# Adding layer 2's direct outputs over the dimensions on GpSimd in place of VectorE, and dealing the gathers out 9, 10, 11, 9 a block

## The chip, the cores and the metric

The kernel runs on one core of a Trainium2 chip. The metric is the device time of one execution in microseconds (us). Three executions of the kernel before took 1320.02, 1320.3 and 1326.73 us, median 1320.3.

## The reference

1024 samples each have 39 ids. Each id picks a row of 16 floats from one of 39 tables, which gives x0 of shape (1024, 39, 16). Three layers follow, all in float32:

```
for idx, (W, b) in enumerate(params):          # W: (39, fields of xk, 128)
    z = einsum('bhd,bkd,hks->bsd', x0, xk, W) + b
    z = relu(z)                                 # (samples, 128 units, 16 dimensions)
    layers 0 and 1: xk = z[:, :64], direct gets z[:, 64:]
    layer 2:        direct gets all 128 units of z
logit = sum(concatenate(direct, axis=1), axis=-1)   # over the 16 dimensions
```

The logit (64 + 64 + 128 = 256 numbers a sample) and 16 dense inputs go through a small network: 272 to 512, 512 to 256, 256 to 1, with relu after the first two.

## The kernel before, in words

**Tiles and blocks.** The samples are cut into 8 blocks of 128. A tile is one block times 4 of the 16 dimensions, so that it has 512 columns (4 dimensions by 128 samples), and there are 32 tiles, t = 0 to 31, 4 to a block. The units lie on the 128 partitions. One body of the loop (37 us) handles tile t: layer 1 of t, layer 0 of tile t + 1, layer 2 of t, and the transposes of the gathered rows for tile t + 2 (AHEAD = 2). Every engine has its own program with the same bodies in the same order (`steps`, line 329): the first bodies are written out, then comes a hardware loop whose turn is 4 bodies, then the rest is written out again. GpSimd's loop has one turn less than the others.

**Products.** In layers 1 and 2 there are 10 steps j = 0 to 9, each of two products of 128 x 512. VectorE multiplies (line 687) and TensorE contracts (line 789). The table KINDS says how a step reaches TensorE:

```
KINDS = {1: "UVPPUPVPVP", 0: "UUUU", 2: "UUVUPUVPUP"}
```

A U step goes to TensorE as it is, as two float32 matmuls. A V or P step is split in a rounded head (ScalarE, line 559) and a rest, which is the product minus its head; then TensorE makes six shorter matmuls. The rest of a V step is made by VectorE (line 694), the rest of a P step by GpSimd (line 464). So GpSimd makes the rests of j = 2, 3, 5, 7, 9 of layer 1 and of j = 4, 7, 9 of layer 2. TensorE takes the steps in order and waits for each P step on `s_rest_p`.

**The queue of GpSimd.** Between its rests, GpSimd issues the gathers of a later block, one indirect DMA for each of the 39 fields (`gather`, line 449), into the tile `gathered`. GATHERS_OF_TILE says how many a body issues, by k = (t + 2) mod 4, and GATHERS_AFTER how many of them may follow the n-th rest of a layer; what is left over goes after the last rest of layer 2:

```
GATHERS_AFTER = {1: (0, 1, 0, 0, 7), 2: (1, 2, 2)}
GATHERS_OF_TILE = (11, 12, 12, 4)
```

So a body with t mod 4 = 2 has k = 0 and 11 gathers, t mod 4 = 3 has 12, t mod 4 = 0 has 12 and t mod 4 = 1 has 4. In the body with k = 0, GpSimd first waits until ScalarE has copied the previous block's rows away, and copies the new block's indices (`refill`, line 504, `new_indices`, line 444). That body gathers nothing before the last rest of layer 1. From t = 26 on there is nothing left to gather. ScalarE waits for all 39 gathers of a block at line 573, in layer 1 of the body with t mod 4 = 2.

**The direct outputs.** ScalarE writes relu(z) of layer 2, transposed in its access pattern, to 4 of the 16 dimensions of `direct2` (128 units x 128 samples x 16 dimensions; `out_layer2`, line 563, called in layer 1 of the next body). When the 4 tiles of a block are in, VectorE adds the 16 dimensions with one tensor_reduce over 2048 columns and writes 128 columns of `sum2`:

```
def add_dims(out, direct, t, done):
    nc.vector.tensor_reduce(cols, direct[:], AX_X, ALU.add).then_inc(done, 1)
```

For layer 2 this is `add_layer2` (line 720). It stands in the body of VectorE with t mod 4 = 0, between the products of layer 0 and the wait for layer 2's input x2 (`s_x2`), for t = 4 to 28, and once more at the end of its program. The directs of layers 0 and 1 have `add_layers01` (line 724), in layer 2 of the body with t mod 4 = 3, after step j = 7; it is not touched. Two others wait for `s_sum2`: ScalarE, before it writes the first tile of the next block into `direct2` (line 566, in layer 1 of the body with t mod 4 = 1), and TensorE in the network at the end (line 857), where the first 512 samples need 4 sums and the second 512 need all 8.

Of the kernel before, what the change touches and what calls it, by code (L numbers as in the profile page):

```python
# [8 lines left out]
ALU = mybir.AluOpType  # L9
# [3 lines left out]
P = 128  # L13
FIELDS = 39
# [20 lines left out]
PE_ORDER = {1: (0, 1, 2, 3, 4, 5, 6, 7, 8, 9), 2: (0, 1, 2, 3, 4, 5, 6, 7, 8, 9)}  # L35
WHOLE_SLOTS = 6
SPLIT_SLOTS = 4
GATHERS_AFTER = {1: (0, 1, 0, 0, 7), 2: (1, 2, 2)}
GATHERS_OF_TILE = (11, 12, 12, 4)
GATHERS_EARLY = (20, 10, 9)  # L40
D2_AFTER = 6
XT_AFTER = 3
# [7 lines left out]
TOGETHER = TPB  # L50
D0_AFTER = 5
AHEAD = 2


class Tile:
# [30 lines left out]
def build_kernel(nc, dense_ctx, ids, tables, W_top1, b_top1, W_top2, b_top2, W_top3,  # L86
# [3 lines left out]
    TILES = BLOCKS * TPB  # L90
# [14 lines left out]
    with ExitStack() as ctx:  # L105
# [6 lines left out]
        def sem(name):  # L112
            return ctx.enter_context(nc.semaphore(name))
# [28 lines left out]
        idx = sb("idx", [P, FIELDS], I32)  # L142
# [61 lines left out]
        s_select = sem("first_shift_selected")  # L204
        s_ids = sem("ids_loaded")
        s_idx = sem("idx_ready")
        s_gather = sem("gather_landed")
        s_emb = sem("emb_ready")
        s_x0 = sem("x0_transposed")
        s_xt = sem("xt_ready")  # L210
# [13 lines left out]
        s_d01 = sem("direct01_ready")  # L224
        s_d2 = sem("direct2_ready")
        s_sum01 = sem("sum01_ready")
        s_sum2 = sem("sum2_ready")
        s_ctx_t = sem("ctx_transposed")
        s_ctx = sem("ctx_ready")
# [83 lines left out]
        def stage(t, layer):  # L313

            if t.turn is None and t.first < 0:
                return 0
            last = t.turn is None and t.first == TILES - 1
            return t.count(3, {1: 1, 0: 2, 2: 3}[layer] - (1 if last and layer == 2 else 0))

        def z_of(t, layer):  # L320
            return z[stage(Tile(t.first), layer) % 2]

        REPEATED = [[0, HALF], [2 * N, CPL], [1, N]]

# [4 lines left out]
        def steps(eng, body, turns=TURNS):  # L329

            for t in range(-AHEAD, LOOP0):
                body(Tile(t))
            with eng.Fori(0, turns) as turn:
                for k in range(TPB):
                    body(Tile(LOOP0 + k, turn))
            for t in range(LOOP0 + turns * TPB, TILES):
                body(Tile(t))
# [104 lines left out]
        @block.gpsimd  # L442
        def _(pool):
            def new_indices(b):

                src = idx_all[:, b, :] if isinstance(b, int) else idx_all[:, bass.ds(b, 1), :]
                nc.gpsimd.tensor_copy(idx[:], src).then_inc(s_idx, 1)

            def gather(f):

                nc.gpsimd.indirect_dma_start(  # L451
                    gathered[:, f, :], None, tables[f],
                    bass.IndirectOffsetOnAxis(ap=idx[:, f:f + 1], axis=0)).then_inc(s_gather, 16)

            def rests(t, layer, fields, refill=None):

                split = [j for j, kind in enumerate(KINDS[layer]) if kind == "P"]
                for n, j in enumerate(split):
                    product = t, layer, j
                    if j == split[-1] and refill is not None:  # L460
                        refill()
                        refill = None
                    pool.wait_ge(s_head, before(t, layer, j, "PV") + 1)
                    nc.gpsimd.tensor_tensor(rest[:, split_slot(product)], whole_slot(product),  # L464
                                            head[:, split_slot(product)].bitcast(F32),
                                            ALU.subtract).then_inc(s_rest_p, 1)
                    for _ in range(GATHERS_AFTER[layer][n] if refill is None else 0):
                        if fields:
                            gather(fields.pop(0))
                while layer == 2 and fields:  # L470
                    gather(fields.pop(0))

            pool.wait_ge(s_ids, 16)
            new_indices(0)
            pool.wait_ge(s_idx, 1)
            for f in range(FIELDS):
                if f == FIELDS // 2:
                    pool.wait_ge(s_ident0, 1)
                    nc.gpsimd.affine_select(out=ident[:], in_=ident[:], compare_op=ALU.not_equal, fill=1.0,
                                            base=0, pattern=[[-1, P]], channel_multiplier=1).then_inc(s_ident, 1)  # L480
                gather(f)
            pool.wait_ge(s_emb, 1)
            new_indices(1)
            pool.wait_ge(s_idx, 2)
            early = list(range(FIELDS))
            for f in early[:GATHERS_EARLY[0]]:
                gather(f)
            del early[:GATHERS_EARLY[0]]
            def body(t):
                if not has_layers12(t):  # L490
                    return
                ahead = t.plus(AHEAD)
                k = ahead.first % TPB
                refill = None
                if t.turn is None and t.first < LOOP0:
                    fields = early[:GATHERS_EARLY[1 + t.first]]
                    del early[:GATHERS_EARLY[1 + t.first]]
                elif t.turn is None and ahead.blocks(1, 1) >= BLOCKS:
                    fields = []
                else:  # L500
                    first = sum(GATHERS_OF_TILE[:k])
                    fields = list(range(first, first + GATHERS_OF_TILE[k]))
                    if k == 0:
                        def refill():

                            pool.wait_ge(s_emb, ahead.blocks(1, 1))
                            new_indices(ahead.blocks(1, 1))
                            pool.wait_ge(s_idx, ahead.blocks(1, 2))
                rests(t, 1, fields, refill)
                rests(t, 2, fields)  # L510

            steps(pool, body, TURNS - 1)

        @block.scalar
        def _(act):
# [53 lines left out]
            def transposed(t):  # L569
                nxt = t.plus(AHEAD)  # L570
                if nxt.first % TPB == 0:

                    act.wait_ge(s_gather, nxt.blocks(16 * FIELDS, 16 * FIELDS))
                    wait(act, s_x0, nxt.count(1))
                    nc.scalar.copy(emb[:], gathered[:].rearrange("p f d -> p (f d)").unsqueeze(1)
                                   .to_broadcast([P, SPC, FIELDS * DIM])).then_inc(s_emb, 1)
                act.wait_ge(s_x0, nxt.count(1, 1))
                wait(act, s_stored, nxt.count(32, -32))
                nc.scalar.copy(xt[:, nxt.first % 2, :],
                               x0_bank[nxt.first % 2][0:FIELDS, :]).then_inc(s_xt, 1)  # L580
# [63 lines left out]
        def _(dve):  # L644
# [69 lines left out]
            def add_dims(out, direct, t, done):  # L714

                b = t.blocks()
                cols = out[:, b * P:(b + 1) * P] if t.turn is None else out[:, bass.ds(b * P, P)]
                nc.vector.tensor_reduce(cols, direct[:], AX_X, ALU.add).then_inc(done, 1)  # L718

            def add_layer2(t):  # L720
                dve.wait_ge(s_d2, t.count(1, 1))
                add_dims(sum2, direct2, t, s_sum2)

            def add_layers01(t):
                dve.wait_ge(s_d01, t.count(2, 2))
                add_dims(sum01, direct01, t, s_sum01)
# [1 line left out]
            def body(t):  # L728
                if has_layers12(t):
                    dve.wait_ge(s_x1, t.count(2, 2))  # L730
                    layer12(t, 1, x1_bank, {})
                if has_layer0(t):
                    nxt = t.plus(1)
                    dve.wait_ge(s_xt, nxt.count(1, 1))
                    wait(dve, s_shift, nxt.count(16 * SPC))
                    for j in range(PAIRS0):
                        c = slice(2 * j, min(2 * j + 2, CHUNKS0))
                        if has_layers12(t):
                            product(t, 0, j, x0_bank[nxt.first % 2], x_shift[:, c, :], ROWS0)
                        else:  # L740
                            dve.wait_ge(s_first, 1)
                            dve.wait_ge(s_select, j + 1)
                            product(t, 0, j, x_shift[:, 0, :],
                                    first_shift[j][0:ROWS0, 0:c.stop - c.start, :], ROWS0)
                if has_layers12(t):
                    if t.first % TOGETHER == 0 and (t.turn is not None or t.first > 0):
                        add_layer2(t.plus(-1))
                    dve.wait_ge(s_x2, t.count(2, 2))
                    ends = t.first % TOGETHER == TOGETHER - 1
                    layer12(t, 2, x2_bank, {ADD_01_AFTER: lambda: add_layers01(t)} if ends else {})  # L750

            steps(dve, body)
            add_layer2(Tile(TILES - 1))

        @block.tensor
        def _(pe):
# [134 lines left out]
```

## Time and profile before

| | |
|---|---|
| median of three executions | 1320.3 us |
| the profiled execution | 1325.62 us |
| its span, first to last instruction | 1323.8 us |
| mean granted clock of TensorE | 0.996 of full speed |
| TensorE busy | 1247.7 us, 94% |
| VectorE busy | 1090.1 us, 82% |
| GpSimd busy | 910.8 us, 69% |
| ScalarE busy | 663.1 us, 50% |
| 256 rests by GpSimd | 609.9 us |
| 312 gathers issued by GpSimd | 299.0 us |
| 16 sums over the dimensions by VectorE (8 of them layer 2's) | 36.4 us |

How to read it: PE is TensorE's matmuls, PEld its weight loads (they overlap the matmuls), DVE is VectorE, ACT ScalarE, POOL GpSimd, SP SyncE. Busy time leaves out waits, register instructions and the issue of DMAs by the queues of SP and ACT. A busy share says how full an engine is over the whole span. Whether it holds the others up is to be read from the stretch in question.

### The profile page before, as it was taken

The numbers are of one execution on the slowest core, as the hardware profiler recorded it, in microseconds if no ns is written. First come the engines' busy times: TensorE is split into PE (matmuls) and PEld (weight loads), VectorE is DVE, ScalarE is ACT, GpSimd is POOL, SyncE is SP. The second block draws the span as 40 slices with busy tenths as digits, with TensorE's granted clock in tenths as the row PEclk, the third lists the DMA queues.
The fourth block names the chain that finished last, engine by engine and source line by source line (L and its number), as shares of the span: only waits on it lengthen the run. The fifth ranks groups of instructions, "written<-read, shape, count | busy, mean of one in ns | idle before, by whom it ended". The sixth has DMA issues, their size and how long they took to land.

```text
span 1323.8 us, 15099 instructions
## 1 busy us (share of the span) xinstructions
PE 1247.7 (94%) x4078; PEld 768.8 (58%) x4078; DVE 1090.1 (82%) x965; ACT 663.1 (50%) x704; POOL 910.8 (69%) x581
## 2 busy tenths in 40 slices
PE   0289999999999999999999999999999999999989
PEld 0136666666656666666655666666666666666633
DVE  1149888989999888988998888989999888989850
ACT  1124555545554555556554555555554555555532
POOL 6668778876888678876886678886888655555520
PEclk9999999999999999999999999999999999999999
DMA  6198777787887777887897677878887777777500
GB/s 184 27 217 206 178 192 183 201 195 191 214 191 181 178 187 195 190 196 193 211 211 179 144 189 192 193 197 201 216 182 175 188 190 185 192 191 190 128 0 0
DMA packets 133859, 233.49 MB, mean 176 GB/s; under 512 B 15890, under 2 KB 23043, under 8 KB 133729
## 3 DMA queue, kind: packets, MB, share of 16 engines
q1 hardware_dynamic: 80333, 146.77, 47.5%
q10 hardware_dynamic: 43522, 83.90, 24.2%
q0 software_dynamic: 9984, 2.58, 2.2%
q8 instruction: 9, 0.15, 0.0%
q14 instruction: 11, 0.09, 0.0%
HBM read 229.33 MB, written 6.23 MB: 178 GB/s over the span
## 4 chain that ended last, share of the span: by engine, by line
PE 76%; POOL 10%; issue 7%; DVE 6%; ACT 1%; DMA 0%; DVEq 0%; POOLq 0%; ACTq 0%
PE z_odd L789 32%; PE z_even L789 28%; PE z_even L796 7%; POOL gathered L451 6%; POOL rest L464 5%; PE z_odd L796 4%; DVE whole L687 3%; PE whole_psum L869 2%; DVE rest L694 1%; DVE whole_psum L687 1%; PE x_even L816 1%; PE x_odd L816 1%; PE x_odd L869 1%; PE x_even L869 1%; DVE sum L718 1%
## 5 line engine op out<-in xcount | busy, mean ns | idle before, releaser
L464 POOL TENSOR_TENSOR rest<-whole,head 128x1024 fp32r<-128x1024 f32 x256 | 609.9, 2394 | 274.9 <-ACT head L559 273.8
L687 DVE TENSOR_TENSOR whole<-x_banks,x_rep 128x1024 f32<-128x1024 f32 x480 | 567.2, 1212 | 89.3 <-ACT x_banks L528 86.3
L559 ACT CAST head<-whole 128x1024 fp32r<-128x1024 f32 x256 | 268.8, 1050 | 202.9 <-DVE whole L687 139.2
L451 POOL DMA_INDIRECT gathered<-in_tbl,idx x312 | 299.0, 958 | 86.7 <-issue 77.6
L789 PE MATMUL z_odd<-whole,w_whole 128*128 128x512 f32 x468 | 219.8, 598 | 5.5 <-DVE whole L687 5.5
L559 ACT CAST head<-whole_psum 128x1024 fp32r<-128x1024 f32 x160 | 162.3, 1014 | 122.3 <-DVE whole_psum L687 115.5
L694 DVE TENSOR_TENSOR rest<-whole_psum,head 128x1024 fp32r<-128x1024 f32 x160 | 194.6, 1216 | 22.8 <-ACT head L559 22.6
L789 PE MATMUL z_odd<-head,w_rest 128*128 128x512 f32 x426 | 198.2, 465 | 6.1 <-POOL rest L464 3.4
L687 DVE TENSOR_TENSOR whole_psum<-x_banks,x_rep 128x1024 f32<-128x1024 f32 x160 | 195.9, 1224 | 8.7 <-DMA x_rep<-x_rows 7.2
L789 PE MATMUL z_even<-whole,w_whole 128*128 128x512 f32 x428 | 198.5, 592 | 0.0
L789 PE MATMUL z_even<-head,w_rest 128*128 128x512 f32 x406 | 186.1, 458 | 5.9 <-DVE rest L694 4.2
L789 PE MATMUL z_odd<-rest,w_head 128*128 128x512 f32 x426 | 167.2, 393 | 0.0
L789 PE MATMUL z_odd<-head,w_head 128*128 128x512 f32 x426 | 166.9, 392 | 0.0
L789 PE MATMUL z_even<-rest,w_head 128*128 128x512 f32 x406 | 158.9, 391 | 0.0
L789 PE MATMUL z_even<-head,w_head 128*128 128x512 f32 x406 | 158.6, 391 | 0.0
L789 PEld LDWEIGHTS z_odd<-whole,w_whole 128*128 128x128 f32 x468 | 89.2, 191 | 87.3 <-issue 75.2
L789 PEld LDWEIGHTS z_even<-whole,w_whole 128*128 128x128 f32 x428 | 80.8, 189 | 72.1 <-issue 65.5
L796 PE MATMUL z_even<-whole,w0s 117*128 117x512 f32 x238 | 111.8, 621 | 0.0
L789 PEld LDWEIGHTS z_odd<-head,w_rest 128*128 128x128 f32 x426 | 80.5, 189 | 50.6 <-POOL rest L464 17.6
L789 PEld LDWEIGHTS z_even<-head,w_rest 128*128 128x128 f32 x406 | 76.5, 189 | 46.7 <-issue 12.2
L789 PEld LDWEIGHTS z_odd<-head,w_head 128*128 128x128 f32 x426 | 80.5, 189 | 29.5 <-issue 15.6
L796 PE MATMUL z_odd<-whole,w0s 117*128 117x512 f32 x210 | 92.6, 592 | 0.0
(74 smaller groups left out, 876.9 us busy)
## 6 DMA issues: line engine op xcount, KB each, us to landing
x_rep<-x_rows SPq DMA_DIRECT2D x160, 512.0 KB, 10.7
x_rep<-x_rows ACTq DMA_DIRECT2D x160, 512.0 KB, 11.4
x_shift<-x_rows SPq DMA_DIRECT2D x93, 546.0 KB
gathered<-in_tbl,idx POOLq DMA_INDIRECT x312
x_rows<-xt_and_ctx SPq DMA_DIRECT2D x32, 78.0 KB
x_rows<-xt_and_ctx SPq DMA_DIRECT2D x32, 40.0 KB
x_rep<-in_W_top SPq DMA_DIRECT2D x2, 512.0 KB, 12.0
w_k<-in_L_rec_w SPq DMA_DIRECT2D x1, 760.5 KB
```

The lines of the kernel that those rows point to most:

```text
L451: nc.gpsimd.indirect_dma_start(gathered[:, f, :], None, tables[f], bass.IndirectOffsetOnAxis(ap=idx[:, f:f + 1], axis=0)).then_inc(s_gathe ...
L464: nc.gpsimd.tensor_tensor(rest[:, split_slot(product)], whole_slot(product), head[:, split_slot(product)].bitcast(F32), ALU.subtract).then ...
L559: nc.scalar.copy(head[:, split_slot(product)], src).then_inc(s_head, 1)
L687: nc.vector.tensor_tensor(out[0:rows, 0:width, :], xk[0:rows, :].unsqueeze(1).to_broadcast([rows, width, N]), x0, ALU.mult).then_inc(s_pro ...
L694: nc.vector.tensor_tensor(rest[:, split_slot(product)], whole_psum[:], head[:, split_slot(product)].bitcast(F32), ALU.subtract).then_inc(s ...
L718: nc.vector.tensor_reduce(cols, direct[:], AX_X, ALU.add).then_inc(done, 1)
L789: mm = nc.tensor.matmul(zz[:], w, x, start=(j == PE_ORDER[layer][0] and i == 0), stop=(j == PE_ORDER[layer][-1] and i == len(terms) - 1))
L796: mm = nc.tensor.matmul(z_of(t, 0)[:], w0s[0:ROWS0, i, :], whole_slot((t, 0, j))[0:ROWS0, i - 2 * j, :], start=(i == 0), stop=(i == CHUNKS ...
L816: mm = nc.tensor.transpose(out[0:ROWS0, i * P:(i + 1) * P], rows, ident[:])
L869: mm = nc.tensor.matmul(out, w, x, start=(i == 0), stop=(i == len(terms) - 1))
```

## The change

It does three things. The layer-2 sum moves from VectorE's program to GpSimd's: there it is four in-place additions, which fold 16 dimensions into 8, 4, 2 and 1, each waiting for the one before on the new semaphore `s_halved`. It stands in the body with t mod 4 = 0, for t = 4 to 28, after the rest of layer 2's first P step (j = 4), and once more at the end of GpSimd's program. The gathers are dealt out anew. And a block's 39 gathers count on four semaphores (12, 12, 8 and 7 fields) where they counted on one; ScalarE waits for all four in the place where it waited for the one.

```
-GATHERS_AFTER = {1: (0, 1, 0, 0, 7), 2: (1, 2, 2)}
-GATHERS_OF_TILE = (11, 12, 12, 4)
+GATHERS_AFTER = {1: (0, 1, 0, 0, 8), 2: (0, 1, 4)}
+GATHERS_OF_TILE = (9, 10, 11, 9)
+GATHER_GROUPS = (12, 12, 8, 7)
...
+        s_halved = sem("dims_halved")
...
+        def wait_gathers(eng, t, groups):
+            for g in groups:
+                eng.wait_ge(s_gather[g], t.blocks(16 * GATHER_GROUPS[g], 16 * GATHER_GROUPS[g]))
...
-                    bass.IndirectOffsetOnAxis(ap=idx[:, f:f + 1], axis=0)).then_inc(s_gather, 16)
+                    bass.IndirectOffsetOnAxis(ap=idx[:, f:f + 1], axis=0)).then_inc(s_gather[group_of[f]], 16)
...
+            def add_layer2(t):
+                b = t.blocks()
+                cols = sum2[:, b * P:(b + 1) * P] if t.turn is None else sum2[:, bass.ds(b * P, P)]
+                pool.wait_ge(s_d2, t.count(1, 1))
+                for n, width in enumerate((8, 4, 2)):
+                    if n:
+                        pool.wait_ge(s_halved, t.blocks(3, n))
+                    nc.gpsimd.tensor_tensor(direct2[:, :, 0:width], direct2[:, :, 0:width],
+                                            direct2[:, :, width:2 * width], ALU.add).then_inc(s_halved, 1)
+                pool.wait_ge(s_halved, t.blocks(3, 3))
+                nc.gpsimd.tensor_tensor(cols, direct2[:, :, 0], direct2[:, :, 1], ALU.add).then_inc(s_sum2, 1)
...
                     nc.gpsimd.tensor_tensor(rest[:, split_slot(product)], whole_slot(product),
                                             head[:, split_slot(product)].bitcast(F32),
                                             ALU.subtract).then_inc(s_rest_p, 1)
+                    if (layer, n, t.first % TOGETHER) == (2, 0, 0) and (t.turn is not None or t.first > 0):
+                        add_layer2(t.plus(-1))
                     for _ in range(GATHERS_AFTER[layer][n] if refill is None else 0):
...
             steps(pool, body, TURNS - 1)
+            add_layer2(Tile(TILES - 1))
...
-                    act.wait_ge(s_gather, nxt.blocks(16 * FIELDS, 16 * FIELDS))
+                    wait_gathers(act, nxt, range(len(GATHER_GROUPS)))
...
-            def add_layer2(t):
-                dve.wait_ge(s_d2, t.count(1, 1))
-                add_dims(sum2, direct2, t, s_sum2)
...
-                    if t.first % TOGETHER == 0 and (t.turn is not None or t.first > 0):
-                        add_layer2(t.plus(-1))
                     dve.wait_ge(s_x2, t.count(2, 2))
...
             steps(dve, body)
-            add_layer2(Tile(TILES - 1))
```

## Rows read from the trace of the kernel before

**Rows 1.** The page, section 1: busy time and share of the span of each engine.

```profile
PE 1247.7 (94%) x4078; PEld 768.8 (58%) x4078; DVE 1090.1 (82%) x965; ACT 663.1 (50%) x704; POOL 910.8 (69%) x581
```

**Rows 2.** Busy time by stretch, each from one layer 0 to the next.

```profile
core 0: us, PE busy (x) PEld busy (x) DVE busy (x) ACT busy (x) POOL busy (x), PEclk, DMA share, GB/s
254.89:293.69 38.80, 37.15 (x126) 23.24 (x125) 33.68 (x30) 19.80 (x21) 30.45 (x21) 1.00 0.79 188
515.17:552.85 37.68, 37.07 (x126) 23.24 (x125) 35.99 (x31) 19.78 (x21) 30.48 (x21) 1.00 0.83 190
552.85:589.68 36.83, 36.83 (x125) 23.31 (x124) 33.68 (x30) 19.79 (x21) 30.46 (x21) 1.00 0.82 194
589.68:626.30 36.62, 36.62 (x125) 23.40 (x124) 32.60 (x29) 21.47 (x22) 22.09 (x13) 1.00 0.80 192
626.30:663.17 36.87, 36.87 (x126) 23.31 (x125) 32.69 (x29) 19.79 (x21) 30.52 (x21) 1.00 0.81 194
700.86:742.27 41.41, 38.56 (x126) 24.30 (x125) 33.67 (x30) 19.79 (x21) 30.46 (x21) 0.96 0.73 172
```

**Rows 3.** Timeline of TensorE, layer 2 of tile 12: start us, us, what.

```profile
569.89 0.39 PE L789 MATMUL z_odd<-head,w_rest 128*128 128x512 f32 x1
...
571.26 1.88 PE L789 MATMUL z_odd<-whole,w_whole 128*128 128x512 f32 x4
573.11 0.50 PE L789 MATMUL z_odd<-head,w_rest 128*128 128x512 f32 x1
```

**Rows 4.** Timeline of GpSimd in the same body, and the next one's start.

```profile
551.33 0.96 POOL L451 DMA_INDIRECT gathered<-in_tbl,idx  x1
...
558.83 0.94 POOL L451 DMA_INDIRECT gathered<-in_tbl,idx  x1 [0.30 <-issue]
561.40 2.40 POOL L464 TENSOR_TENSOR rest<-whole,head 128x1024 fp32r<-128x1024 f32 x1 [1.62 <-ACT head L559]
...
565.92 2.37 POOL L464 TENSOR_TENSOR rest<-whole,head 128x1024 fp32r<-128x1024 f32 x1 [1.03 <-ACT head L559]
...
570.68 2.37 POOL L464 TENSOR_TENSOR rest<-whole,head 128x1024 fp32r<-128x1024 f32 x1
...
574.18 4.74 POOL L464 TENSOR_TENSOR rest<-whole,head 128x1024 fp32r<-128x1024 f32 x2
```

**Rows 5.** Timeline of VectorE in the same body: the sum, and layer 2's first products.

```profile
551.57 2.28 DVE L718 TENSOR_REDUCE sum<-direct 128x2048 f32 x1
554.49 2.36 DVE L687 TENSOR_TENSOR whole<-x_banks,x_rep 128x1024 f32<-128x1024 f32 x2 [0.65 <-ACT x_banks L528]
```

**Rows 6.** Groups by line and shape: count | busy us, mean ns of one | idle before.

```profile
L464 POOL TENSOR_TENSOR rest<-whole,head 128x1024 fp32r<-128x1024 f32 x256 | 609.9, 2394 | 274.9 <-ACT head L559 273.8
L447 POOL COPY idx<-idx_all 128x39 int32 x6 | 1.3, 222 | 0.0
L718 DVE TENSOR_REDUCE sum<-direct 128x2048 f32 x14 | 31.8, 2274 | 0.0
L528 ACT ACTIVATE direct<-z_odd,bias 128x512 f32<-128x512 f32 x17 | 19.4, 1139 | 4.2 <-PE z_odd L789 4.2
L528 ACT ACTIVATE x_rep<-whole_psum,bias_t 128x512 f32<-128x512 f32 x6 | 4.1, 687 | 14.2 <-PE whole_psum L869 14.2
```

**Rows 7.** Waits of GpSimd: who waited for whom, us in total, times, longest.

```profile
POOL gathered L451 <- POOL idx L447: 0.6, 2, 0.3
```

**Rows 8.** The chain of work that ended last, from 706 us to 724 us.

```profile
711.80 5.50 issue
```

**Rows 9.** Timeline of TensorE: its first matmul after two waits.

```profile
286.75 0.50 PE L789 MATMUL z_even<-head,w_rest 128*128 128x512 f32 x1 [1.65 <-POOL rest L464]
...
720.92 0.80 PE L789 MATMUL z_odd<-head,w_rest 128*128 128x512 f32 x1 [2.85 <-POOL rest L464]
```

**Rows 10.** Busy time by stretch, columns as in rows 2: just after the second wait.

```profile
720.90:724.30 3.40, 3.38 (x7) 2.48 (x8) 2.06 (x2) 0.36 (x1) 2.95 (x3) 0.50 1.06 267
```

**Rows 11.** The end: the last sum, and the network's first matmul for samples 512 on.

```profile
1281.66 2.29 DVE L718 TENSOR_REDUCE sum<-direct 128x128 f32<-128x2048 f32 x1 [6.41 <-ACT direct L528]
...
1292.27 1.12 PE L869 MATMUL whole_psum<-xt_and_ctx,x_rep 16*128 16x512 f32 x2
```

More of the change, by code:

```diff
@@ L206, in build_kernel @@
         s_idx = sem("idx_ready")
-        s_gather = sem("gather_landed")
+        s_gather = [sem(f"gather_landed_{g}") for g in range(len(GATHER_GROUPS))]
         s_emb = sem("emb_ready")
@@ L321, in z_of @@
             return z[stage(Tile(t.first), layer) % 2]
+        group_of = [g for g, size in enumerate(GATHER_GROUPS) for _ in range(size)]
+        def wait_gathers(eng, t, groups):
+            for g in groups:
+                eng.wait_ge(s_gather[g], t.blocks(16 * GATHER_GROUPS[g], 16 * GATHER_GROUPS[g]))
         REPEATED = [[0, HALF], [2 * N, CPL], [1, N]]
```

## The prediction

> **What bounds the kernel now.** The page comes first: TensorE is busy for 94% of the span, VectorE for 82%, GpSimd for 69% [rows 1]. That is an average, so the second view is the busy time by stretch, cut from one layer 0 to the next, which holds layer 2 of one tile and layer 1 of the next [rows 2]. The shortest stretch is 36.62 us and TensorE is busy for all of it: that is TensorE's own work, and nobody can make a tile cheaper than that. A block is four such stretches. In the middle of the run they take 37.68, 36.83, 36.62 and 36.87 us [rows 2], so only 1.06 + 0.21 + 0 + 0.25 = 1.5 us in 148 are not TensorE's. The kernel is bound by TensorE, and this change leaves TensorE's work as it is. It can win only out of those 1.5 us a block, and it can lose whatever it makes TensorE wait, since a stretch with no spare time behind it gives nothing back.
>
> Third, the timelines of TensorE, GpSimd and VectorE around the place of the change, layer 2 of tile 12 [rows 3 to 5]. TensorE takes up step j = 7 at 569.89 us. GpSimd had its rest ready at 565.92 + 2.37 = 568.29, which is 1.6 us in hand. For j = 9 the rest ends at 570.68 + 2.37 = 573.05 and TensorE begins at 573.11, though it could have begun at 572.98 (j = 8 starts at 571.26 and is two matmuls of 0.86 us, half of a shown pair each): there GpSimd is just too late [rows 3, 4]. So GpSimd, at 69% of the span, is the engine next in line in exactly this place.
>
> **VectorE loses the sum.** It gives up 8 reductions of 2.27 us [rows 6], 18 us of busy time. The one in the body of tile 12 runs from 551.57 to 553.85; then VectorE still stands idle for 0.65 us until ScalarE delivers x2, and begins layer 2 at 554.49 [rows 5]. Without the sum it stands idle for 2.9 us and begins at 554.49 all the same. The sum has its cover in that wait, so I cost its removal at 0. If x2 came 0.65 us sooner or more, it would count. The stretch with 1.06 us lost is the one with layers 0 and 1's sum (VectorE is busy for 35.99 us in it, against 33.68 in its neighbour [rows 2]); that sum stays.
>
> **GpSimd gains four additions.** They work on 128 x 8 = 1024, 512, 256 and 128 columns, 1920 in all. The trace has one kind of addition or subtraction on GpSimd, 1024 columns in 2394 ns, or 2.34 ns a column [rows 6]: 1920 columns are 4.49 us. A start is contained in that once. The copy of 39 columns takes 222 ns [rows 6], of which 0.09 are columns, so a start is 0.13 us, and three more are 0.4 us. Each of the three waits for the addition before it is like the one wait of this kind in the trace, an instruction after the index copy, 0.3 us [rows 7]: 0.9 us. Together T = 5.8 us. **Low bound:** columns alone, 4.49 us (starts overlap, waits cost nothing). **High bound:** these operands step over memory, 8, 4, 2 and 1 columns out of every 16, and no row has GpSimd doing so. The nearest is ScalarE, which takes 1139 ns where it writes 512 columns into `direct` by strides and 687 ns where it writes 512 in a row [rows 6], 1.66 times as long. That gives 4.49 x 1.66 + 1.3 = 8.7 us. I take 5.8, since GpSimd's own row is nearer than another engine's.
>
> The Trainium skill (GPSIMD Engine Reference, section 7, performance pitfalls) says that reading with a step over 8 bytes costs GpSimd about half as much again per element; here only the last addition, of 128 columns, steps so. No row shows it. As an estimate from that page the last addition would be 0.15 us longer, seven times, and the sum 1 us higher.
>
> **What stands behind them.** Queued behind the additions are the rests of j = 7 and j = 9, and TensorE waits for both. In tile 12: 8 gathers in place of 7 begin at 551.33, 1.25 us apart ((558.83 - 551.33) / 6), and end at 561.0; the rest of j = 4 was waiting for its head until 561.40, so the eighth gather is hidden [rows 4], with 0.4 us to spare. That rest ends at 563.80. The additions run to 569.6, the rest of j = 7 to 571.97, and TensorE starts j = 7 at 572.0 in place of 569.89: **2.1 us late**. It would be on time only for T up to 569.89 - 0.05 - 2.37 - 563.80 = 3.7 us. TensorE then wants j = 9 at 572.0 + 1.37 + 1.72 = 575.1. GpSimd issues one gather, which puts 1.13 us between two rests (573.05 to 574.18 [rows 4]), and ends the rest at 571.97 + 1.13 + 2.37 = 575.47; TensorE starts at 575.5, **2.4 us after** the 573.11 of before. The wait for `s_d2` is for a relu done a layer earlier. ScalarE and VectorE, which wait for slots, wait for TensorE and so shift with it. Into layer 1 of tile 13 GpSimd goes as before: it was the last at j = 9 then too, one gather follows in both versions, and the two rests after it start 0.07 us behind TensorE's last wait as they did [rows 3, 4].
>
> **The gathers.** In the body with t mod 4 = 2 one gather used to follow the last rest of layer 2, and now none does, and layer 2 has one gather less between the rests. The stretch with that loses 0.25 us [rows 2] and should lose none. In the one with t mod 4 = 3 a gather goes in the same place, but its 1.06 us are VectorE's: 0. The body with t mod 4 = 1 now issues 8 gathers before j = 4 of layer 2, in a gap of which the old 3 used under half: 0. ScalarE's three more waits a block are for gathers issued half a body earlier: 0; if they landed late, the emb copy would be late next. Four semaphores change no instruction of GpSimd: 0.
>
> **The end.** The last sum ran from 1281.66 to 1283.95, and TensorE needs it at 1292.27 [rows 11], for the second half of the samples. On GpSimd it ends at 1287.4: hidden with 4.8 us to spare, even at 8.7 us.
>
> **The sum.** Six blocks (t = 4 to 24) pay 2.4 us: 14.4. At t = 28 there are no gathers left, so only j = 7 is late: 2.1. Six stretches win 0.25: -1.5. Together **+15.0 us**; at T = 4.49 it is 6 x 1.1 + 0.8 - 1.5 = +5.9, at T = 8.7 it is 6 x 5.3 + 5.1 - 1.5 = +35.4. The profiled execution, 1323.8 us of span and 1.8 around it, took 1325.6 and would become 1340.6. It stands 5.3 us over the median, and the trace says why: GpSimd's queue stood still twice with nothing to wait for, once for 5.5 us [rows 8], which made two stretches 38.80 and 41.41 us long in place of 36.83 [rows 2], 6.5 us in all. The median has none of it, so I add to the median: 1320.3 + 15.0 = **1335.3 us**.
>
> **The rivals.**
> The additions fit (10%). The place is one body's gap after j = 4; below T = 3.7 us TensorE waits for nothing new and the six quarter microseconds are won: 1318.8 us, not slower. It needs 1.9 ns a column with starts and waits in it. Against it stand 256 rests at 2.34; for it, only that no short addition is in the trace.
> VectorE's time comes out (4%). If layer 2's start hung on the sum, seven of 2.27 us would be saved, 1320.3 - 15.9 = 1304.4. The idle 0.65 us behind the sum speaks against it [rows 5].
> The clock (15%). After a wait of 2.85 us TensorE ran at a granted 0.50, its 1.2 GHz level, for 3.4 us; after one of 1.65 us it did not slow [rows 9, 10]. That cost 38.56 - 36.83 = 1.7 us of busy time [rows 2]. My wait of 2.1 us lies between. If each of the seven brings it: 1335.3 + 11.9 = 1347.2 us. I leave it out of the sum because 2.1 is nearer to 1.65.
> Strides are dear on GpSimd too (10%): 1355.7 us.
> The queue stops again (5%). A longer GpSimd program may stop in every one of its six turns as it did in two, 3.2 us each: 1354 us.
> Half of the last three cases, and all between, lies under 1352.
>
> **How the numbers follow.** My forecast has the remaining 56%, with 1326 to 1346 as its own range. A measurement of this kernel can tell about 0.5% from no change, so same is 1313.7 to 1326.9 us. Faster: the VectorE rival and a sliver, 5%. Same: the first rival and the lower edge of the forecast, 17%. Slower: the rest, 78%. The range, 1324 to 1352, leaves out the two rivals below it and about half of the dearest cases.
>
> **What would show it.** Right: layer 2 of a tile with t mod 4 = 0 has four additions of about 2.4, 1.3, 0.7 and 0.4 us on GpSimd, TensorE waits there for GpSimd's rest by about 2 us and again by 0.4, that stretch takes 39.2 us, the one two later 36.62, VectorE waits 2.9 us for x2, and GpSimd's busy time is 39 us longer. Wrong: a stretch of 36.8 us there, a clock under 1.00 in it, additions over 7 us in all, or a wait of ScalarE for gathers.

## The result, and the profile after

The changed kernel takes 1325.12 us (median of 20 runs), the kernel before 1322.45 us (median of 20): the ratio is 1.0021, 95% interval 1.0012 to 1.0030. That is 2.7 us slower where I had forecast 15.0. With 20 runs of each the difference is clear of noise, and it lies within the 0.5% that I called no change. The sign was right and the size was not. The time itself lies just inside my range of 1324 to 1352 us, but the range stood on a median of three runs (1320.3) that was 2.1 us below the one of 20.

The stretches first, from one layer 0 to the next as in [rows 2], in the profile of the changed kernel (its span is 1322.4 us):

```profile
core 0: us, PE busy (x) PEld busy (x) DVE busy (x) ACT busy (x) POOL busy (x), PEclk, DMA share, GB/s
250.55:288.97 38.42, 37.22 (x126) 23.24 (x124) 32.69 (x29) 19.80 (x21) 34.07 (x24) 1.00 0.79 187
511.55:549.26 37.71, 37.10 (x125) 23.24 (x124) 34.79 (x30) 19.80 (x21) 28.56 (x19) 1.00 0.82 189
549.26:587.67 38.41, 37.17 (x126) 23.23 (x125) 32.69 (x29) 19.79 (x21) 34.07 (x24) 1.00 0.79 186
587.67:624.29 36.62, 36.62 (x126) 23.40 (x125) 32.69 (x29) 21.46 (x22) 26.77 (x18) 1.00 0.80 194
624.29:660.91 36.62, 36.62 (x126) 23.40 (x125) 32.69 (x29) 19.84 (x21) 28.61 (x19) 1.00 0.80 195
698.60:737.01 38.41, 37.16 (x126) 23.23 (x125) 32.62 (x29) 19.80 (x21) 34.06 (x24) 1.00 0.79 186
1146.70:1184.60 37.90, 36.91 (x125) 23.32 (x124) 32.69 (x29) 19.79 (x21) 23.55 (x12) 1.00 0.77 186
```

Read them against [rows 2]. The stretch with the additions (third line) has grown from 36.83 to 38.41 us, 1.58. The one two later has lost its quarter microsecond (36.87 to 36.62). VectorE's own is as it was (37.68 and 37.71), and t = 28, without gathers, has gone from 36.62 to 37.90. Six times 1.58, and 1.28, less six times 0.25, is **+9.3 us**. But the first and the sixth line do not fit that sum: they stand for 38.80 and 41.41 us of before, and they are shorter now, not longer. The two long standstills of GpSimd's queue are gone. They cost (38.80 - 36.83) + (41.41 - 36.83) = 6.5 us, and 9.3 - 6.5 = 2.8 us, where the medians differ by 2.7. From layer 0 of tile 1 to its end the profiled execution takes 1216.7 us before (1323.8 - 107.1) and 1219.4 after (1322.4 - 103.0), 2.7 us more.

The additions, in the timeline of GpSimd in the same body as [rows 4]: start, us, what.

```profile
556.48 0.94 POOL L460 DMA_INDIRECT gathered<-in_tbl,idx  x1 [0.30 <-issue]
557.81 2.39 POOL L486 TENSOR_TENSOR rest<-whole,head 128x1024 fp32r<-128x1024 f32 x1 [0.39 <-ACT head L584]
560.16 4.41 POOL L472 TENSOR_TENSOR direct<-direct 128x1024 f32<-128x1024 f32 x3
564.75 0.42 POOL L475 TENSOR_TENSOR sum<-direct 128x128 f32 x1 [0.19 <-POOL direct L472]
565.12 2.38 POOL L486 TENSOR_TENSOR rest<-whole,head 128x1024 fp32r<-128x1024 f32 x1
567.65 0.96 POOL L460 DMA_INDIRECT gathered<-in_tbl,idx  x1
568.64 2.39 POOL L486 TENSOR_TENSOR rest<-whole,head 128x1024 fp32r<-128x1024 f32 x1
```

The eighth gather has gone into the wait for the head, which is down from 1.62 to 0.39 us. From the end of that rest (560.20) to the next (565.12) are T = 4.92 us. TensorE waits twice, for the rest of j = 7 and for the rest of j = 9:

```profile
567.56 0.50 PE L807 MATMUL z_odd<-head,w_rest 128*128 128x512 f32 x1 [1.09 <-POOL rest L486]
...
571.08 0.50 PE L807 MATMUL z_odd<-head,w_rest 128*128 128x512 f32 x1 [0.15 <-POOL rest L486]
```

And the additions by shape (count | busy us, mean ns of one | idle before):

```profile
L472 POOL TENSOR_TENSOR direct<-direct 128x1024 f32<-128x1024 f32 x8 | 18.8, 2356 | 2.9 <-ACT direct L553 2.9
L472 POOL TENSOR_TENSOR direct<-direct 128x512 f32<-128x512 f32 x8 | 10.2, 1279 | 0.6
L472 POOL TENSOR_TENSOR direct<-direct 128x256 f32<-128x256 f32 x8 | 4.9, 612 | 0.6
L475 POOL TENSOR_TENSOR sum<-direct 128x128 f32 x6 | 2.5, 416 | 1.1 <-POOL direct L472 1.1
```

Together 4.66 us a block. 1024 columns in runs of eight take 2356 ns, no more than the contiguous rest, 2394 [rows 6]. By the column it is 2.30, 2.50, 2.39 and 3.25 ns; the last, of single columns 16 apart, has the start on only 128 columns. My sum for it without dearer steps was 0.13 + 0.30 = 0.43 us, and it took 0.42, so the 0.15 us more that I had estimated for its steps does not show. (By the line through 1024 and 256 columns 128 would take 0.32 us; even so no more than 0.1 us could be theirs.) VectorE, without its sum, stands idle that much longer and starts layer 2 no earlier (timeline of VectorE; 0.65 us of idle time in [rows 5]):

```profile
550.91 2.35 DVE L712 TENSOR_TENSOR whole<-x_banks,x_rep 128x1024 f32<-128x1024 f32 x2 [2.84 <-ACT x_banks L553]
```

### The profile page after: what moved, and what is told of

Same layout as the page of the kernel before. It is cut to its first block, busy times and chain, and to the rows that moved or that the text cites. A ratio compares the mean times of both kernels' runs of the same rounds, so it can differ in the third digit from the quotient of the medians.

```text
span 1322.4 us, 15169 instructions
## 1 busy us (share of the span) xinstructions
PE 1243.4 (94%) x4078; PEld 767.1 (58%) x4078; DVE 1072.6 (81%) x957; ACT 663.2 (50%) x704; POOL 946.0 (72%) x613
## 4 chain that ended last, share of the span: by engine, by line
PE 49%; POOL 32%; issue 13%; DVE 3%; ACT 1%; DMA 0%; POOLq 0%; DVEq 0%; ACTq 0%
PE z_even L807 22%; POOL rest L486 16%; PE z_odd L807 16%; POOL gathered L460 13%; PE z_odd L814 4%; PE z_even L814 3%; POOL direct L472 2%; DVE whole L712 2%; PE whole_psum L887 2%; DVE whole_psum L712 1%; PE x_even L887 1%; PE x_odd L887 1%; ACT head L584 1%; PE x_odd L834 1%; PE x_even L834 1%
## 5 line engine op out<-in xcount | busy, mean ns | idle before, releaser
L814 PE MATMUL z_even<-whole,w0s 117*128 117x512 f32 x238 | 109.1, 609 | 0.0
```

The lines of the kernel that those rows point to most:

```text
L814: mm = nc.tensor.matmul(z_of(t, 0)[:], w0s[0:ROWS0, i, :], whole_slot((t, 0, j))[0:ROWS0, i - 2 * j, :], start=(i == 0), stop=(i == CHUNKS ...
```

## The experiments

Ratios are to the kernel before on the same chip, with their 95% intervals; on different chips that kernel took 1322 to 1328 us.

**Was it luck?** A stop, or standstill, is here an idle time of GpSimd in front of a gather for which the profile names no cause ("issue"). My sum took the two standstills for the luck of one execution. Two profiles more, without an edit:

> The kernel before once more, unchanged, for a second profile of it. Theory A (the 6.5 us of queue stops on GpSimd and the late full clock at the start are luck of one execution): the stretches of 36.83, 36.62, 36.87 and 37.70 us come back, the two stops of 2.4 and 5.7 us on GpSimd are gone or stand elsewhere, and the start (first layer 0 of tile 1, at 107 us before) moves by up to 4 us. Theory B (they belong to the program of before): stops in the same tiles (t = 4 and 16), 6 to 7 us in all, and layer 0 of tile 1 at 107 us again.

> The changed kernel once more, unchanged, for a second profile. Theory A (luck of one execution): stretches of 38.4 us again, and now stops on GpSimd's queue or a start later by up to 4 us may be there. Theory B (the change takes the stops away): no stop over 0.4 us on GpSimd again, and layer 0 of tile 1 begins at 103 us again.

Theory B held for the stops, theory A for the start. Before once more: the same two tiles, stretches of 38.79 and 40.81 us. After once more: no idle time of that kind over 0.3 us before any of the 312 gathers, in both profiles of after (who waited for whom; us in total, times, longest; first before again, then after):

```profile
POOL gathered L451 <- issue: 77.9, 257, 5.1
```

```profile
POOL gathered L460 <- issue: 77.7, 271, 0.3
```

The stop comes in front of the same two gathers in both profiles of before, the 114th and the 227th of the program, which is 113 and 2 x 113 gathers issued. In the first profile of before (timeline of GpSimd):

```profile
275.28 0.96 POOL L451 DMA_INDIRECT gathered<-in_tbl,idx  x1 [0.16 <-issue]
276.26 4.73 POOL L464 TENSOR_TENSOR rest<-whole,head 128x1024 fp32r<-128x1024 f32 x2
283.34 0.97 POOL L451 DMA_INDIRECT gathered<-in_tbl,idx  x1 [2.35 <-issue]
```

In the packets of the gathers' queue, all packets of the gathers so far had landed when it went on. But landing is not all of it: the last packet ended at 280.88 us, GpSimd was free at 280.99 and began the gather at 283.34. In front of the 227th the last packet ended at 714.55 and the gather began at 717.52. So 2.4 and 3.0 us of the two stops come when no gather is in flight any more.

The layer 0 of tile 1 began at 107.09 and 105.37 us before and at 102.98 and 101.23 after. In the other kernels' profiles it lies from 103.2 to 108.7. The four profiles with the new deal have the four lowest values (101.2 to 104.8, the others from 105.4 up), so a relation is not ruled out. Between before and after it does not count on average, though: the medians differ by 2.7 us, as the rest of the run does without the start.

**The sum alone.** GATHERS_AFTER, GATHERS_OF_TILE and the one semaphore as before, the additions as in the change:

```
-GATHERS_AFTER = {1: (0, 1, 0, 0, 8), 2: (0, 1, 4)}
-GATHERS_OF_TILE = (9, 10, 11, 9)
-GATHER_GROUPS = (12, 12, 8, 7)
+GATHERS_AFTER = {1: (0, 1, 0, 0, 7), 2: (1, 2, 2)}
+GATHERS_OF_TILE = (11, 12, 12, 4)
+GATHER_GROUPS = (39,)
```

> The sum on GpSimd as in the change, but the gathers dealt as before (11, 12, 12, 4 and the old places) on one semaphore. If GpSimd's queue sets it: two gathers more stand between the additions and the rest of j = 9 than in the change, so TensorE waits about 2.3 us for j = 7 and 1.7 us more for j = 9; the stretch of t mod 4 = 0 takes 40.7 us in place of 38.41, six times, and the kernel 1345 to 1348 us, some 22 us over the kernel before. Rival, that a late rest costs the run less than its stretch shows (the change cost 2.7 us by the medians and 9.3 by its stretches): about 1329 us.

Measured: 1348.19 us, ratio 1.0185 (1.0167 to 1.0202), 24.5 us over before and just above the 1345 to 1348 expected. Stretches of the profile (columns as above):

```profile
254.28:297.21 42.93, 37.48 (x125) 23.15 (x124) 32.69 (x29) 19.80 (x21) 35.08 (x25) 1.00 0.69 169
408.38:449.40 41.02, 37.20 (x126) 23.23 (x125) 32.70 (x29) 19.80 (x21) 35.05 (x25) 1.00 0.74 174
560.58:601.58 41.00, 38.53 (x125) 24.28 (x124) 32.69 (x29) 19.80 (x21) 35.05 (x25) 0.96 0.74 174
```

41.0 us against the 40.7 expected: counting the queue in front of each rest gives the wait of TensorE, here 2.47 us for j = 7 and 1.36 for j = 9 (timeline of TensorE in the second of the stretches):

```profile
428.05 0.50 PE L807 MATMUL z_odd<-head,w_rest 128*128 128x512 f32 x1 [2.47 <-POOL rest L486]
...
432.80 0.50 PE L807 MATMUL z_odd<-head,w_rest 128*128 128x512 f32 x1 [1.36 <-POOL rest L486]
```

The first stretch has a stop on top, in front of the 114th gather again (2.06 us). The one at the 227th took 3.01 us, though by then the last packet had long ended, at 726.14, before GpSimd had finished the additions (timeline of GpSimd):

```profile
728.32 0.43 POOL L475 TENSOR_TENSOR sum<-direct 128x128 f32 x1 [0.28 <-POOL direct L472]
731.75 0.96 POOL L460 DMA_INDIRECT gathered<-in_tbl,idx  x1 [3.01 <-issue]
```

So the new deal of the gathers is what makes the sum on GpSimd bearable: it saves 2.6 us a block in that body.

**The new deal alone**, on the kernel before, one semaphore:

```
-GATHERS_AFTER = {1: (0, 1, 0, 0, 7), 2: (1, 2, 2)}
-GATHERS_OF_TILE = (11, 12, 12, 4)
+GATHERS_AFTER = {1: (0, 1, 0, 0, 8), 2: (0, 1, 4)}
+GATHERS_OF_TILE = (9, 10, 11, 9)
```

> The new deal of the gathers (9, 10, 11, 9) alone: one semaphore, the sum on VectorE. If a gather between two rests is what costs the quarter microseconds: the stretches that took 36.83 and 36.87 us take 36.62, 12 in all, so 2.8 us less, about 1319.7 us, a ratio of 0.998. Rival, that the deal also takes away the stops of GpSimd's queue: 1315 us or less, 0.995. Rival, that VectorE's idle time matters: no difference.

Measured: 1323.91 us, ratio 1.0012 (1.0003 to 1.0021). None of the three. The stretches of 36.83 and 36.87 us did all become 36.62, as the first said. But the profile has a longer stop, once (timeline of GpSimd):

```profile
289.58 0.95 POOL L451 DMA_INDIRECT gathered<-in_tbl,idx  x1 [0.30 <-issue]
300.41 0.95 POOL L451 DMA_INDIRECT gathered<-in_tbl,idx  x1 [9.88 <-issue]
```

It is again the 114th gather. Now it stands in the middle of a row of eight, its neighbours in front have only just been issued, and GpSimd stands still for 9.88 us: 6.6 until they have landed (the last packet ended at 297.14) and 3.3 more. That stretch took 45.71 us, of which 1.6 are matmuls at a lower clock (TensorE busy for 38.23 us, mean granted clock 0.93). No second stop shows at the 227th. All gathers before it had landed, at 732.63 against 737.58, but so they had at the 227th of the sum alone, which stopped; why this one did not is open. So how long the stop is depends on where the program has its 114th gather, and the deal does not take it away. What does, in the change, was left: the semaphores.

**The semaphores**, taken out of the changed kernel, and put alone into the kernel before:

```
-GATHER_GROUPS = (12, 12, 8, 7)
+GATHER_GROUPS = (39,)
```

> The changed kernel with its 39 gathers a block on one semaphore again, nothing else. Theory S (on one semaphore GpSimd stops before its 114th and its 227th gather until all earlier gathers have landed; four semaphores take that away): the 114th gather stands in the middle of a row of eight, as in the kernel with the new deal alone, so a stop of about 9.9 us comes back there in tile t = 5 and costs some 8 to 9 us: 1333 to 1335 us. Theory P (the place of a gather in the program decides, not the semaphore): no stop, 1325 us as the change.

```
-                    bass.IndirectOffsetOnAxis(ap=idx[:, f:f + 1], axis=0)).then_inc(s_gather, 16)
+                    bass.IndirectOffsetOnAxis(ap=idx[:, f:f + 1], axis=0)).then_inc(s_gather[group_of[f]], 16)
...
-                    act.wait_ge(s_gather, nxt.blocks(16 * FIELDS, 16 * FIELDS))
+                    wait_gathers(act, nxt, range(len(GATHER_GROUPS)))
```

The second has GATHER_GROUPS = (12, 12, 8, 7) and `wait_gathers` as in the change.

> The kernel before with the four semaphores alone. Theory S: both stops (2.35 and 5.1 to 5.7 us) are gone, the two stretches of 38.8 and 40.8 to 41.4 us take 36.87, and the kernel is 6 us faster, 1316 us, a ratio of 0.9955. Theory P: stops before the 114th and 227th gather as before, 1322.5 us.

Measured: the changed kernel on one semaphore 1338.97 us, ratio 1.0100 (1.0082 to 1.0118), against 1.0021 with four, so 10 us for the one stop (its stretch takes 46.96 us in place of 36.62, of which 2.8 are matmuls at a lower clock, 0.89 on average); the kernel before on four semaphores 1318.93 us, ratio **0.9948** (0.9932 to 0.9965). Theory S on both sides (on this chip the kernel before takes 1326.55 us). The 114th gather of the first (timeline of GpSimd), and all waits of that kind in the second (longest 0.3 us):

```profile
303.86 0.95 POOL L460 DMA_INDIRECT gathered<-in_tbl,idx  x1 [9.96 <-issue]
```

```profile
POOL gathered L459 <- issue: 71.3, 260, 0.3
```

The stretches of the second are 36.87 and 36.90 us where 38.80 and 41.41 had stood.

**Two semaphores**, to learn what is counted (against the version just above):

```
-GATHER_GROUPS = (12, 12, 8, 7)
+GATHER_GROUPS = (20, 19)
```

> The kernel before with two gather semaphores, 20 and 19 fields. If the stop belongs to each semaphore's own count of 113 gathers (112 to 113 of them fit, then GpSimd waits until all on it have landed): the first group reaches its 114th in block 5 at the 209th gather of all, the second at the 234th, so there is a stop just before each of these, one of them or both costing TensorE some us, and none at the 114th and 227th of all: 1318 to 1326 us. If it is only the number of semaphores that matters (more than one, no stop): no stop anywhere, 1319 us, a ratio of 0.995 as with four. If it is the number of gathers in a row on one semaphore: stops as before.

Measured: 1321.58 us on a chip where the kernel before takes 1327.97, ratio 0.9947 (0.9927 to 0.9967), and no stop in front of any gather, the 209th and the 234th included. So it is not a count of 113 on each semaphore. Two semaphores are enough here. What GpSimd waits for at its 114th gather on one, and why a second semaphore frees it, stays open.

**The additions where GpSimd has room.** Between the last rest of layer 1 and the first of layer 2 lie 10.1 us [rows 4], filled with gathers. Here the additions take the place of four of these:

```
-GATHERS_AFTER = {1: (0, 1, 0, 0, 8), 2: (0, 1, 4)}
-GATHERS_OF_TILE = (9, 10, 11, 9)
+GATHERS_AFTER = {1: (0, 1, 0, 0, 8), 2: (1, 1, 1)}
+GATHERS_OF_TILE = (11, 12, 8, 8)
...
-                    if (layer, n, t.first % TOGETHER) == (2, 0, 0) and (t.turn is not None or t.first > 0):
-                        add_layer2(t.plus(-1))
-                    for _ in range(GATHERS_AFTER[layer][n] if refill is None else 0):
+                    gathers = GATHERS_AFTER[layer][n]
+                    if (layer, j, t.first % TOGETHER) == (1, split[-1], 0) and (t.turn is not None or t.first > 0):
+                        add_layer2(t.plus(-1))
+                        gathers = 4
+                    for _ in range(gathers if refill is None else 0):
```

> The sum on GpSimd right after the rest of the last P step of layer 1 (t mod 4 = 0), followed by 4 gathers in place of 8, before anything of layer 2 is due; gathers dealt 11, 12, 8, 8, one after each rest of layer 2; four semaphores. The gap there is 10.1 us, the additions and four gathers take 9.7. By theory A (TensorE pays only what GpSimd is late) no stretch is over 36.7 us but the one with VectorE's own sum, 37.7: 9.3 + 1.5 us under the change, about 1314 us, a ratio of 0.994 to before. Rival, that additions on GpSimd slow other engines or are paid for wherever they stand: 1322 us or more.

Measured: 1316.10 us, ratio 0.9935 (0.9910 to 0.9960). Of four stretches three take 36.62 us and the fourth 37.7. So the additions in themselves cost nothing; their place did. The gain over the kernel before is not theirs either: four semaphores alone gave 0.9948, and the rest is the quarter microseconds of 12 stretches, 3.0 us.

**Both sums on GpSimd.** The fourth stretch holds VectorE's sum of layers 0 and 1. This one moves it too, and deals the gathers 11, 8, 8, 12 in place of 11, 12, 8, 8 (against the version just above):

```
+            def add_layers01(t):
+                pool.wait_ge(s_d01, t.count(2, 2))
+                fold(t, sum01, direct01, s_halved01, s_sum01)
...
+                    ends = (layer, j, t.first % TOGETHER) == (1, split[-1], TOGETHER - 1)
+                    if ends:
+                        gathers = 4
...
+                    if ends:
+                        add_layers01(t)
...
-                    layer12(t, 2, x2_bank, {ADD_01_AFTER: lambda: add_layers01(t)} if ends else {})
+                    layer12(t, 2, x2_bank, {})
```

> As the kernel before this one in the list, and the sum of layers 0 and 1 on GpSimd too, in the same four additions, in the gap behind layer 1 of the body with t mod 4 = 3, after 4 gathers and once its last output is written; gathers 11, 8, 8, 12. If VectorE's sum behind step 7 is what makes that stretch 37.70 us: it takes 36.62 to 36.7, eight times 1.07 us less, 1305 to 1306 us, a ratio of 0.987. Rival: the additions start only when ScalarE has written layer 1's outputs, end too late for the rest of j = 4, and TensorE waits 1 us there instead, 1314 us.

Measured: 1351.72 us (of six runs five took 1348.6 to 1356.1 us and one 3541.8), ratio 1.0189 (1.0165 to 1.0213), over 20 us slower, which neither theory had. The stretch in question did fall to 36.61. But another, from layer 2 of t mod 4 = 1 to layer 1 of t mod 4 = 2, went from 36.62 to 44 us, six times (columns as above):

```profile
291.20:335.28 44.08, 39.50 (x126) 25.15 (x125) 32.73 (x29) 21.49 (x22) 29.69 (x20) 0.92 0.68 162
```

The waits of ScalarE and of TensorE name it:

```profile
ACT emb L615 <- DMA gathered<-in_tbl,idx: 51.6, 7, 21.2
...
PE x_even L845 <- ACT emb L615: 52.9, 7, 25.6
```

One of the seven is the start (21 to 26 us in every kernel). The other six are new, about 5 us each for ScalarE and 4.6 for TensorE. The remaining 2.9 of the 7.5 us that a stretch grew by are matmuls at a lower clock (TensorE busy for 39.50 us in place of 36.62, at 0.92). With 12 gathers in the body with t mod 4 = 1, the last of a block was issued after that body's last rest, and the copy that needs it comes early in the next layer 1. So the next version has the last gather sooner, with nine in the gaps that hold no additions:

```
-GATHERS_AFTER = {1: (0, 1, 0, 0, 8), 2: (1, 1, 1)}
-GATHERS_OF_TILE = (11, 8, 8, 12)
+GATHERS_AFTER = {1: (0, 1, 0, 0, 9), 2: (1, 1, 1)}
+GATHERS_OF_TILE = (12, 8, 8, 11)
```

> Both sums on GpSimd as before, gathers 12, 8, 8, 11 with nine in the gaps without additions and only one in layer 2 of the body with t mod 4 = 1. In the kernel with 11, 8, 8, 12 the last gather of a block was issued after the last rest of that body, and ScalarE waited 51.6 us in all for gathers to land (7 times). If that wait alone made its stretches of 43.7 to 44.1 us: here the last gather is issued some 10 us earlier, those stretches take 36.62 to 38 us, and the kernel 1305 to 1312 us, a ratio of 0.985 to 0.990. Rival, that the ninth gather in a gap delays the rest of j = 4 over its 1.2 us of spare: TensorE waits 0.3 us or more there, 12 times, 1310 to 1314 us. If ScalarE still waits for gathers: over 1330 us.

Measured: 1308.41 us, ratio **0.9854** (0.9832 to 0.9876), 1.5% faster than before and faster than the change too. A block of it:

```profile
364.61:401.22 36.61, 36.61 (x126) 23.44 (x124) 32.70 (x29) 19.80 (x21) 31.77 (x20) 1.00 0.84 194
401.22:437.84 36.62, 36.62 (x125) 23.43 (x124) 32.60 (x29) 19.88 (x21) 30.82 (x22) 1.00 0.81 194
437.84:474.46 36.62, 36.62 (x125) 23.42 (x124) 32.69 (x29) 21.43 (x22) 28.71 (x20) 1.00 0.82 194
474.46:511.08 36.62, 36.62 (x126) 23.43 (x124) 32.70 (x29) 19.82 (x21) 31.50 (x22) 1.00 0.82 196
```

By the profile TensorE is busy in all of it, and the stretches of 44 us are gone, so the late gather was their cause. The steady part of this kernel can't get much shorter without taking work from TensorE.

## Why the prediction was right and wrong

**TensorE bounds the kernel at 36.62 us a stretch:** right, down to the last version. **VectorE's saved time is worth nothing:** right, its idle time went from 0.65 to 2.84 us.

**GpSimd's rests of j = 7 and j = 9 come late:** the mechanism was right, in its place and in both of its waits, and the size was off. The term that was mis-sized is T: I had 5.8 us, the profile has 4.92. Columns and starts were 4.49 + 0.4 = 4.9 in my sum and took 4.66. The three waits between the additions, which I took at 0.3 us each from one wait behind a copy [rows 7], leave 4.92 - 4.66 = 0.26 us in all where I had 0.9. In the changed kernel GpSimd's wait for its own addition just before cost at most 0.2 us. With T = 4.92 my own steps give a stretch 1.5 us longer, and it is 1.58. **The gathers after the last rest:** right, six times 0.25. **The end:** hidden, as said. The last sum was done before 1285.2, and needed at 1290.89 (timelines of GpSimd and TensorE):

```profile
1280.33 4.35 POOL L472 TENSOR_TENSOR direct<-direct 128x1024 f32<-128x1024 f32 x3 [2.94 <-ACT direct L553]
1284.75 0.40 POOL L475 TENSOR_TENSOR sum<-direct 128x128 f32<-128x128 f32 x1
```

```profile
1290.89 1.12 PE L887 MATMUL whole_psum<-xt_and_ctx,x_rep 16*128 16x512 f32 x2
```

So far the sum would have been +9.3 in place of +15.0. That is 5.7 of the 12.3 us that I missed by, and T accounts for it (my own steps with 4.92 give +8.7).

**The step that failed**, beside the size of T, is the one about the standstills: "The median has none of it". I saw 5.3 us between the profiled execution and the median of three, saw two stops of GpSimd's queue that cost 6.5 us, and put the one down to the other. Both belong to the program: they came back in the same tiles in a second profile, and the timed runs without them are faster by as much (0.9948). The 5.3 us were the spread of single runs (1319.84 to 1326.73), whose median over 20 is 1322.45 and not 1320.3. With that went the other half: "Four semaphores change no instruction of GpSimd: 0". They are worth -6.5 us, shown from both sides (1.0100 without them, 0.9948 for them alone). +9.3 - 6.5 is +2.8 us, and +2.7 was measured. I had a rival in which the queue stops more often with the longer program, and none in which a part of the change ends the stops.

One thing is left over. By its stretches the new deal alone should be 0.3 us faster than before, and it measured 1.6 us slower (1.0003 to 1.0021). The start, which varies by several microseconds, may hold that; it isn't shown.

**The clock:** right for this kernel, no stretch under 1.00. In the sum alone TensorE's wait of 2.46 us for j = 7 of one tile was followed by 3.4 us at a granted 0.51, the 1.2 GHz level (580.25 to 583.65; 0.96 over the 41.00 us above), and another turn of the same loop with a wait of 2.47 us had none (1.00 over 41.02). So between 1.65 and 2.85 us, where I looked for a bound, the length of this wait alone does not decide it.

## What to carry to other kernels

An idle time that "waited for nothing that the profile shows" is a term of its own: find out if it comes back at the same instruction in a second profile before calling it noise, and ask which part of a change touches that instruction's queue. Work moved to an engine with spare time on average should go into a gap of its own queue (here 10 us between two layers), not in front of something due: the same four additions came with 24.5 us (the sum alone), 9.3 by the stretches (the change), or nothing, by their place and by what stood around them. When gathers are dealt out anew, count where the last of a set is issued as well as how many stand before each rest.

## What the runs showed that I had not expected

GpSimd's indirect gathers on a single semaphore have a stop in front of the 114th of the program (five profiles of four kernels), and in two of the kernels also in front of the 227th (113 and 226 issued). GpSimd goes on 2.1 to 3.3 us after the last gather so far has landed or, where that had come before GpSimd was free, after it is free. So the stop is 2.1 to 3.0 us where all have landed and up to 10 where the last has only just been issued. With two or four semaphores it did not come at these counts, and that alone made the kernel before 0.5% faster. In the version with both sums and 12 gathers in one body there was a single idle time of 2.4 us before the 294th gather, on four semaphores, which began 8.7 us after all before it had landed; what that was I did not find out. An in-place addition of halves on GpSimd took 2.3 to 2.5 ns a column in runs of 8, 4 and 2 out of 16, as against 2.3 in a row.
